# Layer three's weights applied in stage two of a graph network kernel

## The chip, the cores and the metric

The kernel runs on one core of a Trainium2 chip. The metric is the device time of one launch in microseconds. Three runs of the kernel before are given, and one profiled execution.

## The reference

There are 50000 nodes with 128 features and 100000 directed edges, sorted by their target, of which 50000 are the nodes' own loops. First h = relu(layernorm(x)) goes through three layers, and the result is added to x:

```
agg = segment_sum(h[src], dst) * inv_deg
h   = leaky_relu(agg @ Wl.T + b + h @ Wr.T, 0.01)
```

Then relu(layernorm(x)) goes through one attention layer: scores from two dot products, a softmax over the edges that enter a node, the weighted sum of the neighbours' rows, a bias, and again the residual. All is computed in float32. The edge attributes have no influence on the output.

## The kernel before

The nodes are cut into 196 tiles (NG) of 256 (TILE). After a preparation, which sorts out where each tile's edges lie and writes the first table of features to DRAM, four stages follow: layers one, two and three (`phase` with `ph` 1 and 2, then `phase_3`) and the attention (`phase_c`). Each stage runs once over the 196 tiles, and the next stage's gathers start only when all its table rows have been stored.

Every engine has its own program with the same loop over steps. In step s an engine handles several tiles, each at another point of its way; `s.at(-3)` is the tile three steps back. Semaphores count tiles. `steps(eng, 9, phase)` adds nine late steps in which the last tiles run out.

GpSimd gathers the source rows of the edges that are not loops, 128 rows by one indirect DMA (L635). Neighbouring tiles share a window of edges, so 417 gathers serve 196 tiles, at most twelve tiles ahead (DEEP). VectorE builds for each window a mask of 0 and 1 (L1247), edge by node, three tiles ahead. TensorE multiplies rows by mask (L852, `sums`), which gives the neighbours' sum transposed, feature by node. VectorE adds the tile's own transposed features (`with_own`, L1267) and multiplies by the inverse degree (`mean`, L1273), which SP has loaded from DRAM, copied to all partitions (L493). TensorE then multiplies by the two weight matrices of the layer (L877 and L878). A float32 product shows as two records (passes) in the trace, a transposition as one.

In stages one and two ScalarE adds the bias on the way out of PSUM (L722), VectorE applies the leaky relu (`leaky`, L1278), and TensorE transposes the tile back (L886). ScalarE copies that (L729) and stores both forms: `turned`, feature by node, for the next stage's own term, and `tab`, node by feature, for its gathers. SP loads the own term in stages two and three (L490).

Stage three computes the same sums (L852, L1267, L1273), but its products give node by feature: the bias as a product of three bfloat16 parts with ones (L913), then for each half of the tile the own term and the mean with the tile as the stationary operand (L917, L919). ScalarE copies the result (L747). VectorE applies the leaky relu (L1278), adds x (L1339), takes the layernorm's sums (`stats` L1203, `stats_end` L1212), the reciprocal (`scale`, L1219), adds the attention's bias for later (L1354) and prepares the shift nmr (`shift`, L1224). ScalarE takes the square root (`norm_scale`, L684) and applies the norm with the relu (`norm`, L691). TensorE transposes that (L928) and multiplies it by the attention's weights (L936), ScalarE copies both (L759, L765) and stores them as `tab_c` (L770). SP loads x (L477) and stores the sum x1 (L516).

In the attention stage the masks, scores and sums are built from the rows gathered from `tab_c`. It is changed in one thing only, the form in which x1 is loaded (L534). `pair_rows` lays two neighbouring nodes on a partition, so 1024 contiguous bytes; `node_rows` lays nodes p and p + 128 on partition p, so two pieces of 512 bytes.

Of the kernel before, what the change touches and what calls it, by code (L numbers as in the profile page):

```python
# [5 lines left out]
BF16 = mybir.dt.bfloat16  # L6
# [52 lines left out]
SP = 3  # L59
# [109 lines left out]
def build(nc, x, src, dst, wl1, bl1, wr1, wlh, blh, wrh, w_gat, att_s, att_d, bias, out):  # L169
# [11 lines left out]
    with ctx:  # L181
# [36 lines left out]
        ones_b = sb("ones_b", [P, P], BF16)  # L218
        b_part = sb("b_part", [SP, SP, D], BF16)
        b_rest = sb("b_rest", [SP, 2, D])  # L220
        b_sum = sb("b_sum", [SP, D])
        b_row = sb("b_row", [SP, 2, D], BF16)
        is_part = sb("is_part", [SP, SP])

# [67 lines left out]
        new_h = sage[:, 5632:6656].rearrange("p (r j d) -> p r j d", r=RING, j=2)  # L292
        act = sage[:, 3840:4352].rearrange("p (b j d) -> p b j d", b=2, j=2)
# [8 lines left out]
        mv = sb("mv", [P, 2, GJ, 2])  # L302
        std = sb("std", [P, 2, GJ])
# [54 lines left out]
        ps_agg = [None, bank[0:2], bank[0:3], bank[0:2]]  # L358
        ps_zz = [None, bank[3:5], bank[3:6], bank[3:5]]
        ps_own = [bank[2], bank[5]]  # L360
        ps_n = bank[6:8]
        ps_g = [bank[2], bank[5]]
# [4 lines left out]
        def pair(bk, w=D, stride=D):  # L367

            return bk[:, 0:2 * stride].rearrange("p (j w) -> p j w", j=2)[:, :, 0:w]
# [4 lines left out]
                 "sum_v t_v l_v z_a n_cp sq0 sq1 sq2 sq3 sq4 sq5 sq6 b_v ln_v ln_a rs_v nmr_v h_a tr_done ht_cp dense_done wg_done g_cp st0 st1 st2 "  # L374
# [4 lines left out]
                 "ge_v ge_a ge_m gn_v gn_a "  # L379
                 "gn_m low_g edge_st prep_seq turn_v turn_s chain_v chain_ps shift_g").split()  # L380
# [3 lines left out]
        main = [f"{n}{k}" for n, ring in (("ol", OWN), ("sq", OWN), ("il", RING), ("cl", RING)) for k in range(ring)]  # L384
        S.update((n, S[of]) for n, of in zip(general, main, strict=True))
# [19 lines left out]
        def kept(ph, t, ring):  # L405

            return (ph - 1) * NG + max(t - ring + 1, 0)

# [61 lines left out]
        def fast_sync(eng):  # L470
            def load_x(s):
                ld = S[f"x_ld{s.r}"]
                if s.last:
                    eng.dma_start(xin[0:TAIL // 2, s.r, :, :],
                                  x[N - TAIL:N, :].rearrange("(p j) d -> p j d", j=2)).then_inc(ld, 16)
                else:
                    eng.dma_start(xin[:, s.r, :, :], pair_rows(x, s.t)).then_inc(ld, 16)  # L477
# [1343 lines left out]
```

## Time and profile before

| | before |
|---|---|
| median of 3 runs | 2512.96 us |
| lowest and highest | 2511.53, 2515.49 us |
| span of the profiled execution | 2514.0 us |
| TensorE busy | 1865.3 us, 74% |
| VectorE busy | 1991.2 us, 79% |
| ScalarE busy | 1393.8 us, 55% |
| GpSimd busy | 1648.2 us, 66% |
| mean DMA rate | 232 GB/s |

The span of the profiled execution lies 1.0 us above the median. The shares are averages over stages with different limits, so they have to be read by stage. In the profile's lines the first number is the start in microseconds from the span's start, the next the duration; L852 is a line of the code; the text in brackets gives the idle time of the engine before the instruction, and what ended it.

### The profile page before, as it was taken

Reading aid. Unit: us, or ns where it says so; the run is one execution under the profiler, and the core shown is the slowest. Engines: PE = TensorE matmul, PEld = TensorE weight load, DVE = VectorE, ACT = ScalarE, POOL = GpSimd, SP = SyncE. Lnnn points to the kernel's source line nnn. Section 1 sums busy time; section 2 is a strip of 40 time slices with the busy share of each in tenths; the row PEclk is TensorE's granted clock in tenths of the full one; section 3 lists DMA queues with packets and bytes.
Section 4 is the critical chain, followed back from the end, with each engine's and each line's share of the span. In section 5 each row is a group of like instructions: output and inputs, shape, how many; then the busy total and the mean of one; then the engine's idle time right before and its main releaser. Section 6 shows DMA issues by size and latency. Waiting matters only on the chain. (4 is left out here: it accounts for less than half of the span.)

```text
span 2514.0 us, 49419 instructions
## 1 busy us (share of the span) xinstructions
PE 1865.3 (74%) x12376; PEld 1627.8 (65%) x12376; DVE 1991.2 (79%) x8222; ACT 1393.8 (55%) x3711; POOL 1648.2 (66%) x1706
## 2 busy tenths in 40 slices
PE   0000888888886887888887999999999566666666
PEld 0000777777775777777766888888888456555555
DVE  7988766666664666666656999999999699999999
ACT  3696344444442222222223666666666688888887
POOL 2002777777775777777766777767672577777774
PEclk9999999999998999999998999999999799999998
DMA  6685788888886888888886988888888588887887
GB/s 207 216 296 204 235 249 245 247 249 246 249 248 180 244 253 244 244 251 242 251 231 200 264 263 261 258 256 255 257 256 234 139 205 204 206 202 202 205 203 174
DMA packets 597881, 582.84 MB, mean 232 GB/s; under 512 B 79531, under 2 KB 557349, under 8 KB 597568
## 3 DMA queue, kind: packets, MB, share of 16 engines
q1 hardware_dynamic: 402272, 337.58, 44.7%
q0 software_dynamic: 54208, 112.76, 21.0%
q10 hardware_dynamic: 141120, 129.32, 15.0%
q8 instruction: 107, 1.75, 0.3%
q14 instruction: 174, 1.43, 0.2%
HBM read 372.40 MB, written 207.75 MB: 231 GB/s over the span
## 5 line engine op out<-in xcount | busy, mean ns | idle before, releaser
L635 POOL DMA_INDIRECT rows<-tab,idx x1251 | 1229.4, 983 | 548.7 <-issue 342.6
L852 PE MATMUL bank<-mask,rows 128*128 128x128 f32 (+1 forms) x3528 | 645.6, 320 | 208.9 <-DMA rows<-tab,idx 185.9
L852 PEld LDWEIGHTS bank<-mask,rows 128*128 128x128 f32 x3528 | 543.9, 195 | 286.4 <-issue 165.6
L1267 DVE TENSOR_TENSOR sage<-bank,sage 128x256 f32<-128x256 f32 x588 | 247.2, 420 | 413.2 <-PE bank L852 410.9
L722 ACT ACTIVATE sage<-bank,b_col 128x256 f32<-128x256 f32 x392 | 185.9, 474 | 599.6 <-PE bank L878 599.1
L635 POOL DMA_INDIRECT rows<-tab_c,idx x417 | 398.1, 955 | 181.5 <-issue 115.8
L1247 DVE TENSOR_SCALAR mask<-iota,dcol 128x256 f32<-128x256 f32 (+1 forms) x1251 | 418.8, 365 | 0.1
L953 PE MATMUL bank<-ident,mask 128*128 128x128 f32 x784 | 139.9, 305 | 177.5 <-ACT mask L782 176.8
L1273 DVE TENSOR_TENSOR sage<-sage 128x256 f32<-128x256 f32 x588 | 246.3, 419 | 1.8 <-DMA sage<-inv_d 1.6
L1278 DVE SCALAR_TENSOR_TENSOR sage<-sage 128x256 f32<-128x256 f32 x588 | 243.0, 413 | 4.6 <-ACT sage L722 4.6
L877 PE MATMUL bank<-sage,wcat 128*128 128x256 f32 x784 | 236.9, 384 | 0.0
L878 PE MATMUL bank<-sage,wcat 128*128 128x256 f32 x784 | 236.0, 383 | 0.0
L953 PEld LDWEIGHTS bank<-ident,mask 128*128 128x128 f32 x784 | 90.8, 151 | 208.1 <-ACT mask L782 195.2
L963 PE MATMUL bank<-rows,sage 128*128 128x131 f32 x1568 | 224.3, 290 | 1.4 <-ACT sage L802 1.4
L782 ACT ACTIVATE mask<-cut_w,rows 128x256 f32<-128x256 bf16 (+1 forms) x417 | 181.0, 484 | 61.1 <-issue 39.0
L963 PEld LDWEIGHTS bank<-rows,sage 128*128 128x128 f32 x1568 | 207.6, 205 | 1.6 <-ACT sage L802 1.6
L691 ACT ACTIVATE sage<-sage,nmr,rstd 128x128 f32<-128x128 f32 x392 | 172.2, 486 | 42.9 <-DVE nmr L1224 41.6
L802 ACT ACTIVATE sage<-cut_w,ed 128x256 f32<-128x256 bf16 (+1 forms) x441 | 184.4, 473 | 4.9 <-DVE ed L1475 2.6
L917 PE MATMUL bank<-wcat,sage 128*128 128x128 f32 x784 | 177.3, 308 | 0.0
L886 PEld LDWEIGHTS bank<-ident,sage 128*128 128x128 f32 x784 | 152.9, 196 | 22.8 <-issue 4.9
L878 PEld LDWEIGHTS bank<-sage,wcat 128*128 128x128 f32 x784 | 150.9, 192 | 20.9
L1450 DVE TENSOR_REDUCE mx<-bank 128x2 f32<-128x512 f32 x196 | 132.7, 677 | 33.8 <-PE bank L953 33.4
(219 smaller groups left out, 3276.9 us busy)
## 6 DMA issues: line engine op xcount, KB each, us to landing
sage<-inv_d SPq DMA_DIRECT2D x588, 128.0 KB
turned<-sage ACTq DMA_DIRECT2D x392, 128.0 KB
tab<-sage ACTq DMA_DIRECT2D x392, 128.0 KB
sage<-turned SPq DMA_DIRECT2D x392, 128.0 KB
tab_c<-sage ACTq DMA_DIRECT2D x196, 132.0 KB
own_w<-tab_c SPq DMA_DIRECT2D x196, 132.0 KB, 2.9
tab<-sage SPq DMA_DIRECT2D x49, 512.0 KB, 3.5
xin<-tab SPq DMA_DIRECT2D x196, 128.0 KB
```

Of the source, the lines that this page charges most:

```text
L635: eng.indirect_dma_start(out=rows[:, s.win[w], 0:width], out_offset=None, in_=table, in_offset=bass.IndirectOffsetOnAxis(ap=idx[:, s.w + w ...
L722: eng.activation(new_t[:, o.v, :], ps_zz[ph][o.t % len(ps_zz[ph])][:, 0:TILE], ACT.Identity, bias=b_col[:, ph - 1:ph]).then_inc(S["z_a"], 1)
L802: m = eng.activation(prob[:, o.mw[w], a:b], cut[:, o.win[w], a:b], ACT.Exp, bias=ed[:, o.g, 2 * o.k + w:2 * o.k + w + 1])
L852: m = eng.matmul(to[:, a:b], rows[:, s.win[w], 0:D], mask[:, s.mw[w], c:c + b - a], start=(w == 1), stop=(w == 2))
L877: eng.matmul(to, wcat[:, ph - 1, D:2 * D], own_t[:, o.v, :], start=True, stop=False)
L878: eng.matmul(to, wcat[:, ph - 1, 0:D], agg_t[:, o.r, :], start=False, stop=True).then_inc(S["dense_done"], 1)
L953: m = eng.transpose(ps_z[s.t % 3][:, j * TILE + n * P:j * TILE + (n + 1) * P], score[:, s.mw[j + n], (1 - n) * P:(2 - n) * P], ident[:, :])
L963: m = eng.matmul(ps_o[o.k][:, j * TILE:j * TILE + D + 3], prob[:, o.mw[j + n], (1 - n) * P:(2 - n) * P], rows[:, o.win[j + n], 0:D + 3], s ...
L1247: m = eng.tensor_scalar(to[:, g.mw[w], a:b], io[:, a:b], node, None, ALU.is_equal)
L1267: eng.tensor_tensor(agg_t[:, o.r, :], ps[:, 0:TILE], own_t[:, o.v, :], ALU.add).then_inc(S["sum_v"], 1)
L1273: eng.tensor_tensor(agg_t[:, o.r, :], agg_t[:, o.r, :], inv_b[:, o.r, :], ALU.mult).then_inc(S["t_v"], 1)
L1278: eng.scalar_tensor_tensor(at, at, 0.01, at, ALU.mult, ALU.max).then_inc(S["l_v"], 1)
```

## The change

The mean and the product with a matrix can be exchanged, and so can the leaky relu and a multiplication by a positive number. The change uses both for layer three.

At the end of stage two each tile is multiplied by both of layer three's matrices at once, with the tile as the stationary operand (two float32 products of 256 columns), in place of the two transpositions. The half that belongs to Wl is copied by ScalarE and stored as the table for stage three's gathers. VectorE (`weigh`) takes the half that belongs to Wr, adds the bias, multiplies by the degree and adds the tile's own Wl half (the loop). ScalarE stores this one step later to `turned`.

Stage three then starts a PSUM bank with a product of the identity and this prepared term, and adds the gathered rows with the masks as the stationary operand, four products of 128 columns. The result is the layer's value before the leaky relu, times the degree. VectorE applies the leaky relu and, in one operation for each half, multiplies by the inverse degree and adds x. The sums by `with_own`, the multiplication by `mean`, the load of the inverse degree, the bias product and the four products with weights are gone from this stage, and its tiles run through fewer steps: ScalarE has 8 late steps in place of 11. The degree and its inverse, node by partition, are prepared once between stages one and two, by four transpositions, a copy and a reciprocal. The bias parts that stood between stages two and three go. Stage two's table, x and `tab_c` move by `node_rows`, x1 is loaded by `pair_rows`. The diff, cut to its core (lines between @@ say where a piece stands):

```
+        w_out = sage[:, 6656:8448].rearrange("p (v j d) -> p v j d", v=OWN, j=2)
...
-        ps_agg = [None, bank[0:2], bank[0:3], bank[0:2]]
-        ps_zz = [None, bank[3:5], bank[3:6], bank[3:5]]
+        ps_agg = [None, bank[0:2], bank[0:3]]
+        ps_zz = [None, bank[3:5], bank[3:5]]
...
-        ps_g = [bank[2], bank[5]]
+        ps_p = bank[5:8]
+        ps_y = bank[0:4]
+        ps_g = bank[4:6]
...
@@ SP, load(g) of a tile: @@
-                    wait(eng, S["t_v"], kept(ph, g.t, RING))
-                    eng.dma_start(inv_b[:, g.r, :], inv_d[g.t, :].partition_broadcast(P)
-                                  ).then_inc(S[f"il{g.r}"], 16)
+                    if ph < LAYERS:
+                        wait(eng, S["t_v"], kept(ph, g.t, RING))
+                        eng.dma_start(inv_b[:, g.r, :], inv_d[g.t, :].partition_broadcast(P)
+                                      ).then_inc(S[f"il{g.r}"], 16)
+                    else:
+                        wait(eng, S["x1_v"], g.t - RING + 1)
+                        load_x(g)
...
@@ ScalarE, stages one and two: @@
-                        eng.activation(new_h[:, o.r, :, :], pair(ps_n[o.b], D, D), ACT.Copy).then_inc(S["n_cp"], 1)
-                        store_t(o, ph, S["l_v"])
+                        of = pair(ps_n[o.b], D, D) if ph == 1 else pair(ps_p[o.t % len(ps_p)], D, TILE)
+                        eng.activation(new_h[:, o.r, :, :], of, ACT.Copy).then_inc(S["n_cp"], 1)
+                        if ph == 1:
+                            store_t(o, ph)
                     if s.at(-9).there:
-                        store_h(s.at(-9), ph, S["n_cp"])
-                steps(eng, 9, phase)
+                        store_h(s.at(-9), ph)
+                    if ph > 1 and s.at(-10).there:
+                        store_t(s.at(-10), ph)
+                steps(eng, 9 if ph == 1 else 10, phase)
...
@@ ScalarE, stage three (the copy of the result, then the order of norm and norm_scale): @@
-                o = s.at(-4)
+                o = s.at(-1)
...
-                if s.at(-5).there:
-                    norm_scale(s.at(-5), NSG + s.t - 5)
-                o = s.at(-6)
+                o = s.at(-3)
                 if o.there:
                     wait(eng, S["tr_done"], ka + o.t - 1)
                     norm(o, NSG + o.t, h_c[:, o.b, :, :], x1, o.r)
-                o = s.at(-8)
+                if s.at(-2).there:
+                    norm_scale(s.at(-2), NSG + s.t - 2)
+                o = s.at(-5)
...
-            steps(eng, 11, phase_3)
+            steps(eng, 8, phase_3)
...
@@ TensorE, stage two: @@
+                            wait(eng, S["w_v"], o.t - len(ps_p) + 1)
+                            for j in range(2):
+                                m = eng.matmul(ps_p[o.t % len(ps_p)][:, j * TILE:(j + 1) * TILE], new_t[:, o.v, j * P:(j + 1) * P],
+                                               wcat[:, LAYERS - 1, :], start=True, stop=True)
...
@@ TensorE, stage three: @@
-                    sums(s, LAYERS)
-                o = s.at(-3)
-                if o.there:
-
-                    own_there(eng, o, LAYERS)
-                    eng.wait_ge(S["t_v"], ka + o.t + 1)
-                    eng.wait_ge(S["z_a"], kept(LAYERS, o.t, 2))
-                    to = ps_zz[LAYERS][o.b]
-                    eng.matmul(to[:, 0:TILE], ones_b[0:SP, :], b_row[:, :, :].rearrange("p j d -> p (j d)"),
-                               start=True, stop=False)
+                    own_there(eng, s, LAYERS)
+                    wait(eng, S["z_a"], kept(LAYERS, s.t, len(ps_y)))
+                    to = ps_y[s.t % len(ps_y)]
+                    eng.matmul(to[:, 0:TILE], ident[:, :], own_t[:, s.v, :], start=True, stop=False)
+                    eng.wait_ge(S["mask_done"], ka + s.t + 1)
+                    rows_there(eng, s, LAYERS)
                     for j in range(2):
-                        of_j = to[:, j * D:(j + 1) * D]
-                        eng.matmul(of_j, own_t[:, o.v, :].rearrange("p (n j) -> p j n", j=2)[:, j, :],
-                                   wcat[:, LAYERS - 1, D:2 * D], start=False, stop=False)
-                        m = eng.matmul(of_j, agg_t[:, o.r, :].rearrange("p (n j) -> p j n", j=2)[:, j, :],
-                                       wcat[:, LAYERS - 1, 0:D], start=False, stop=(j == 1))
-                    m.then_inc(S["dense_done"], 1)
+                        for n in range(2):
+                            m = eng.matmul(to[:, j * D:(j + 1) * D], mask[:, s.mw[j + n], (1 - n) * P:(2 - n) * P],
+                                           rows[:, s.win[j + n], 0:D], start=False, stop=(j == 1 and n == 1))
+                    m.then_inc(S["agg_done"], 1)
...
@@ VectorE, stage two, for the tile nine steps back, after leaky: @@
+            def weigh(f):
+                eng.wait_ge(S["n_cp"], NG + f.t + 1)
+                eng.tensor_tensor(t_b[:, f.b, :, :], pair(ps_p[f.t % len(ps_p)], D, TILE, D),
+                                  b_bc[:, LAYERS - 1, :].unsqueeze(1).to_broadcast([P, 2, D]), ALU.add
+                                  ).then_inc(S["b_v"], 1)
+                eng.wait_ge(S["b_v"], f.t + 1)
+                wait(eng, S[f"sq{f.v}"], 16 * (NG // OWN + f.uses(OWN)))
+                for j, n in enumerate(of_node(deg_n, f.t)):
+                    m = eng.scalar_tensor_tensor(w_out[:, f.v, j, :], t_b[:, f.b, j, :], n, new_h[:, f.r, j, :],
+                                                 ALU.mult, ALU.add)
+                m.then_inc(S["w_v"], 1)
...
@@ VectorE, stage three: @@
-                if o.there:
-                    with_own(o, LAYERS)
...
-                    leaky(act[:, f.b, :, :])
                 mask_part(s.at(3), LAYERS, 0)
+                    eng.scalar_tensor_tensor(y, y, 0.01, y, ALU.mult, ALU.max).then_inc(S["y_v"], 1)
+                mask_part(s.at(3), LAYERS, 1)
...
-                    eng.tensor_tensor(x1[:, f.r, :, :], act[:, f.b, :, :], xin[:, f.r, :, :], ALU.add
-                                      ).then_inc(S["x1_v"], 1)
-                mask_part(s.at(3), LAYERS, 1)
-                if o.there:
-                    mean(o, LAYERS)
+                    for j, n in enumerate(of_node(inv_n, f.t)):
+                        m = eng.scalar_tensor_tensor(x1[:, f.r, j, :], act[:, f.b, j, :], n, xin[:, f.r, j, :],
+                                                     ALU.mult, ALU.add)
+                    m.then_inc(S["x1_v"], 1)
+                mask_part(s.at(3), LAYERS, 2)
...
-            steps(eng, 6, phase_3)
+            steps(eng, 3, phase_3)
```

## Rows read from the trace of the kernel before

**Rows 1.** The page's 40 slices of the span, tenths of busy time by engine.

```profile
DVE  7988766666664666666656999999999699999999
...
POOL 2002777777775777777766777767672577777774
```

**Rows 2.** Timeline of GpSimd at stage ends: start, us, instruction, [idle before it <-releaser].

```profile
785.04 0.94 POOL L635 DMA_INDIRECT rows<-tab,idx  x1 [16.81 <-DMA tab<-sage]
...
1311.76 0.94 POOL L635 DMA_INDIRECT rows<-tab,idx  x1 [0.30 <-issue]
1329.98 1.08 POOL L635 DMA_INDIRECT rows<-tab,idx  x1 [17.27 <-DMA tab<-sage]
...
1909.89 0.96 POOL L635 DMA_INDIRECT rows<-tab,idx  x1 [0.30 <-issue]
1965.61 0.94 POOL L635 DMA_INDIRECT rows<-tab_c,idx  x1 [54.76 <-DMA tab_c<-sage]
```

**Rows 3.** Windows: stretch, length, busy by engine (PE, PEld, DVE, ACT, POOL), clock, DMA, GB/s.

```profile
850.00:1300.00 450.00, 366.73 (x2007) 321.38 (x2007) 282.67 (x857) 125.54 (x335) 341.81 (x356) 0.97 0.86 247
1350.00:1450.00 100.00, 98.47 (x668) 84.28 (x667) 97.08 (x418) 59.41 (x178) 75.71 (x80) 1.00 0.86 247
1650.00:1850.00 200.00, 199.55 (x1339) 169.29 (x1338) 194.81 (x837) 127.06 (x384) 140.78 (x136) 1.00 0.88 256
```

**Rows 4.** The sums' line L852 on TensorE, stage two, then three: ns, first and last.

```profile
L852 PE MATMUL bank<-mask,rows x1176: 272/275/767, 791.2 to 1317.7; 128*128 128x256 f32 x196
...
L852 PE MATMUL bank<-mask,rows x1176: 272/275/767, 1336.3 to 1944.6; 128*128 128x256 f32 x196
```

**Rows 5.** Timeline of TensorE, a tile of stage two, then of stage one.

```profile
999.93 1.04 PE L852 MATMUL bank<-mask,rows 128*128 128x256 f32 x6
1000.81 0.60 PE L877 MATMUL bank<-sage,wcat 128*128 128x256 f32 x2
1001.24 0.59 PE L878 MATMUL bank<-sage,wcat 128*128 128x256 f32 x2
...
760.17 0.39 PE L886 MATMUL bank<-ident,sage 128*128 128x128 f32 x2
760.40 0.38 PE L866 MATMUL bank<-ident,xin 128*128 128x128 f32 x2
```

**Rows 6.** Timeline of TensorE, a tile of stage three.

```profile
1655.14 0.41 PE L928 MATMUL bank<-ident,sage 128*128 128x128 f32 x2
1655.41 0.69 PE L936 MATMUL bank<-wg,sage 128*128 128x130 f32 x4
1655.94 0.71 PE L852 MATMUL bank<-mask,rows 128*128 128x256 f32 x3
```

**Rows 7.** Timeline of VectorE, a tile of stage three.

```profile
1653.68 0.41 DVE L1267 TENSOR_TENSOR sage<-bank,sage 128x256 f32<-128x256 f32 x1
1654.02 0.41 DVE L1278 SCALAR_TENSOR_TENSOR sage<-sage 128x256 f32<-128x256 f32 x1
1654.51 0.42 DVE L1339 TENSOR_TENSOR sage<-sage,xin 128x256 f32<-128x256 f32 x1
1654.85 0.36 DVE L1247 TENSOR_SCALAR mask<-iota,dcol 128x256 f32<-128x256 f32 x1
```

**Rows 8.** Timeline of VectorE, attention stage.

```profile
2102.83 0.34 DVE L1463 SCALAR_TENSOR_TENSOR sage<-sage,rden 128x128 f32<-128x128 f32 x1
2103.09 0.35 DVE L1469 SCALAR_TENSOR_TENSOR sage<-sage,rden 128x128 f32<-128x128 f32 x1
```

**Rows 9.** Timeline of ScalarE, stage three.

```profile
1650.31 0.30 ACT L684 ACTIVATE std<-mv,eps 128x2 f32<-128x2 f32 x1 [0.91 <-DVE mv L1212]
1650.81 0.49 ACT L691 ACTIVATE sage<-sage,nmr,rstd 128x128 f32<-128x128 f32 x1 [0.21 <-DVE nmr L1224]
```

**Rows 10.** DMA queues: packets, MB, share; attention stage (2050:2450), then stage two (850:1300).

```profile
q1 hardware_dynamic: 122201, 59.53, 54.2%
...
q10 hardware_dynamic: 48022, 43.73, 28.0%
```

More of the change, by code:

```diff
@@ L407, in kept, with of_node @@
             return (ph - 1) * NG + max(t - ring + 1, 0)
+        def of_node(a, t):
+            u, q = t // 2, t % 2
+            return [a[:, 2 * q + j, u:u + 1] for j in range(2)]
         def node_rows(a, t):
@@ L508, in phase @@
                             load(g)
-                    g = s.at(-2)
-                    if ph == LAYERS and g.there:
-                        wait(eng, S["x1_v"], g.t - RING + 1)
-                        load_x(g)
-                    o = s.at(-6)
+                    o = s.at(-4)
                     if ph == LAYERS and o.there:
@@ L893, in fast_tensor @@
                     eng.wait_ge(S["oc_a"], NG)
+                    for q in range(2):
+                        for j in range(2):
+                            at = (2 * q + j) * HALF
+                            m = eng.transpose(ps_deg[:, at:at + HALF], deg[:, q, j * P:(j + 1) * P], ident[0:HALF, 0:HALF])
+                    m.then_inc(S["dn_ps"], 1)
                     eng.wait_ge(S["sum_v"], NG)
                     eng.wait_ge(S["z_a"], NG)
+                    eng.wait_ge(S["dn_v"], 1)
             ka = (LAYERS - 1) * NG
@@ L1299, in phase @@
                         leaky(new_t[:, f.v, :])
-                steps(eng, 5, phase)
-            for k in range(SP):
-                op(eng.tensor_scalar(is_part[:, k:k + 1], part[0:SP, 0:1], float(k), None, ALU.is_equal))
-            op(eng.tensor_copy(b_rest[:, 0, :], b_bc[0:SP, LAYERS - 1, :]))
-            for k in range(SP):
-                op(eng.tensor_copy(b_part[:, k, :], b_rest[:, k % 2, :]))
-                if k < SP - 1:
-                    op(eng.tensor_tensor(b_rest[:, (k + 1) % 2, :], b_rest[:, k % 2, :], b_part[:, k, :], ALU.subtract))
-            op(eng.tensor_scalar(b_sum[:, :], b_part[:, 0, :], is_part[:, 0:1], None, ALU.mult))
-            op(eng.scalar_tensor_tensor(b_sum[:, :], b_part[:, 1, :], is_part[:, 1:2], b_sum[:, :], ALU.mult, ALU.add))
-            op(eng.scalar_tensor_tensor(b_sum[:, :], b_part[:, 2, :], is_part[:, 2:3], b_sum[:, :], ALU.mult, ALU.add))
-            op(eng.tensor_copy(b_row[:, 0, :], b_sum[:, :]))
-            eng.tensor_copy(b_row[:, 1, :], b_sum[:, :]).then_inc(S["b_v"], 1)
+                    f = s.at(-9)
+                    if ph > 1 and f.there:
+                        weigh(f)
+                if ph > 1:
+                    eng.wait_ge(S["dn_ps"], 1)
+                    op(eng.tensor_copy(deg_n[:, :, :].rearrange("p k u -> p (k u)"), ps_deg[:, 0:4 * HALF]))
+                    op(eng.reciprocal(inv_n[:, :, :], deg_n[:, :, :]))
+                    eng.sem_inc(S["dn_v"], 1)
+                steps(eng, 5 if ph == 1 else 9, phase)
             for r in range(RING):
```

113 lines of the change are left out of this document (60 added, 53 removed).

## The prediction

> **What bounds the kernel now.** I read the page's slices first, then busy time by stage, then the first and last instruction of the queues that could carry a stage, then single steps. The slices show four stretches after the preparation: three stages of the convolution and the attention stage; VectorE is at 6 tenths in the first two and at 9 in the last two, GpSimd at 7 in all but the third, where it falls to 6 [rows 1]. A stage handles 196 tiles with 417 gathers. In stage two the first gather starts at 785.04 and the last at 1311.76 [rows 2]: 526.7 us for 417, 1.266 us each, 2.69 us a tile. One gather takes 0.94 us and the next follows 0.30 us later with nothing to wait for [rows 2], so GpSimd's issue rate sets this stage; TensorE is busy for 366.7 of 450 us, VectorE for 282.7 [rows 3]. TensorE's sums run from 791.2 to 1317.7 [rows 4], 2.70 us a tile, six microseconds behind the gathers.
>
> Stage three is different. Early in it (1350 to 1450) 80 gathers still run in 100 us, but from 1650 to 1850 only 136 in 200 us, while TensorE is busy for 199.55 of 200 us and VectorE for 194.8 [rows 3]. The sums run from 1336.3 to 1944.6 [rows 4], 608.3/195 = 3.12 us a tile: TensorE sets the pace. Behind it stands a drain: the last gather starts at 1909.89, the attention stage's first at 1965.61 after 54.76 us of idle time that the stores of tab_c ended [rows 2]; 34.7 us of this are the backlog and 21.0 us (1944.6 to 1965.6) the run through the late steps.
>
> **TensorE in stage three.** A tile costs now 3.12 us. The change drops the bias product, the four products with layer three's weights (eight passes of 128 columns) and the three sums. It puts in a product of ident with the own term (two passes of 256 columns) and four products mask by rows (eight passes of 128). A product of two 256-column passes takes 0.43 us (1000.81 to 1001.24) [rows 5]; four passes of 128 or 130 columns take 0.53 us (1655.41 to 1655.94), the two transposes 0.27 us before it [rows 6]. New tile, added up: 0.43 + 1.06 (8 × 0.53/4) + 0.27 + 0.53 = 2.29 us. By subtraction from the measured step: 3.12 less 0.88 for the sums (999.93 to 1000.81) [rows 5], 1.06 for the eight passes and 0.21 for the bias (one pass of 256 columns, half of 0.43), plus 0.43 and 1.06: 2.46. Either is under 2.69, so the gathers become the bound.
>
> **VectorE in stage three.** Busy 194.8/200 × 3.12 = 3.04 us a tile [rows 3]. Removed: the PSUM addition L1267 (0.34, to the start of L1278), the multiplication by the inverse degree L1273 (the same shape, 0.34), and the residual addition L1339 (0.34); the 0.49 us between the start of the activation L1278 and L1339 holds 0.15 us of waiting for its result [rows 7], which two masks in between can hide. Added: two multiply-adds of 128 columns; the same form with a pointer scalar starts every 0.26 us in the attention stage (2102.83 to 2103.09) [rows 8], 0.52 us. Sum: 3.04 − 1.02 + 0.52 = 2.54, or 2.39 with the wait gone. Under 2.69, by little.
>
> **ScalarE and the shortened pipeline.** Its work a tile stays (five activations). But its norm now stands ahead of norm_scale of the next tile, and VectorE's shift needs that norm_scale one step later: a loop. Its length: 0.21 from VectorE's nmr to the first norm, at most 2 × 0.49 for the norms, 0.30 for the square root [rows 9], some 0.2 back, and 0.4 for the reciprocal and a 256-column addition (priced as L1267), about 2.1 us. Under 2.69, so I charge nothing. SP now fetches x two tiles ahead of its use and issues own_t behind a wait for x1_v; what is queued behind that wait is the next own_t, needed about three tiles (8 us) later. Nothing charged.
>
> **DMA in stage three.** At 3.12 us a tile and 256 GB/s it moves 799 KB [rows 3]. The copies of the inverse degree (131 KB) go: 668 KB, at 2.69 us 248 GB/s, less than now. Against it, x and tab_c now move in 512- and 528-byte pieces. q1 in the attention stage took 0.542 × 16 × 400 us / 122201 = 28.4 ns for 487 bytes, q10 in stage two 0.280 × 16 × 450 / 48022 = 42.0 ns for 911 bytes [rows 10]; 128 KB in halves is then 256 × 28.4 against 128 × 42.0 ns, 1.9 us more over 16 engines, 0.12 us a tile and transfer. I take no loss of pace; the upper bound is a rival.
>
> Stage three then: 195 × (3.12 − 2.70) = 82 us less in its steady part. The drain has eight late steps in place of eleven; 21.0 us becomes about 17 (bounds 13 and 21). Together **86 us less** (bounds 80 and 91).
>
> **Stage two pays.** TensorE: today 0.88 for the sums, 0.43 and 0.43 for the dense products, 0.23 for two transposes (760.17 to 760.40) [rows 5], 1.97 us. The two transposes become two fp32 products of 256 columns: 1.97 − 0.23 + 0.86 = 2.60 us. VectorE: today 282.7/450 × 2.70 = 1.70 us [rows 3]; weigh adds a 256-column addition from PSUM with a wait for its own result (0.49, as from L1278 to L1339 [rows 7]) and two 128-column multiply-adds (0.52 [rows 8]): 2.71 us. ScalarE keeps two activations and two stores. So three engines now need 2.60, 2.71 and 2.69 us a tile, where one did. The lower bound of the pace is 2.70, no loss; the upper one is 3.0, two more waits of 0.15 us on VectorE on top of 2.71, because weigh also waits for ScalarE's copy and for an old store. I take 2.76, near the slowest engine: 195 × 0.06 = 12 us. The drain gets one step and VectorE's weigh, which the third product back waits for: +3 us on today's 12.3 (1317.7 to 1329.98) [rows 2, 4]. Its third buffer for ps_p costs ps_zz one; dense then waits for ScalarE's copy two tiles back, a step behind. The store of w_out waits for w_v on ScalarE, and the next tile's activation is queued behind it; it is one VectorE step late and covered by two buffers. Nothing charged. Together **15 us more** (bounds 3 and 62).
>
> **Edges at nothing.** The degree's four transposes, copy and 392-column reciprocal stand between stages one and two, where TensorE's first sum of stage two starts 6 us after the first gather (791.2 against 785.04) [rows 2, 4]: up to 3 us hide there. The bias splitting between two and three goes; it lay under the 17.27 us in which GpSimd waited for stores [rows 2], and the rows still come 6 us later. The first own_t is needed at once in stage three; its load runs while the first rows are fetched. The attention stage loads x1 in larger pieces, but is held by its gathers; nothing.
>
> **The sum.** The profiled execution's span is 2514.0 us, 1.0 above the median of the three times, 2512.96. 2514.0 − 86 + 15 = 2443 for such an execution, 2442 as a median.
>
> **A rule that speaks against it.** In stage three's early part the gathers keep 1.25 us each (75.71 us busy for 80) while VectorE is busy for 97.1 of 100 us [rows 3], so a full VectorE did not slow them. The Trainium skill, page "SBUF — State Buffer", section "SBUF: two separate sides", says that VectorE and GpSimd share one pair of ports as a lock, and that descriptors of GpSimd's DMAs can wait for it. Stage two gets three more VectorE operations a tile, two of them with two SBUF inputs, and by that rule its gathers could slow; the trace disagrees so far.
>
> **Rivals.**
> 1. Three full engines in stage two get in each other's way: 3.0 us a tile, 195 × 0.30 + 3 = 62 more in place of 15: 2489. For: 2.60, 2.71 and 2.69 leave no reserve, and waits of VectorE on ScalarE's copy come in. Against: in stage three now two engines run 99.8% and 97% busy together [rows 3]. Chance 0.13.
> 2. The gathers slow, by the lock or by DMA. Small pieces raise DMA's share of 0.88 × 3.12 = 2.75 us a tile less 0.33 for the inverse degree (128 × 42 ns/16) plus 0.24, to 2.66 in 2.69: nearly full. A gather took 0.95 us in early stage three and 1.04 late (75.71/80, 140.78/136) [rows 3]; +0.09 on 834 gathers is 75 us at most, half of it 38: 2481. Against: 248 GB/s is no more than now. Chance 0.13.
> 3. **Slower**: the loop VectorE, ScalarE, VectorE of stage three decides. Today ScalarE takes the square root ahead of its norm; the change puts it behind, so scale of the next tile may find it late. VectorE works in order: it then stands still, and its 2.54 us follow the wait instead of lying beside it. ScalarE's part of the loop is 0.21 + 0.98 + 0.30 = 1.5 us [rows 9]; with 0.65 of it uncovered the step is 3.2 us, and 195 × 3.2 + 21 + 6 = 651 us lie between the first gather and the next stage's in place of 635.6: with stage two's 15, 2544. It decides from 3.04 us a tile on (195 × 3.04 + 27 = 635.6 − 15). For: scale is reached only some 2 us after the shift that lets the norm go (2.54 less the 0.5 for addition and shift). Against: these 2 us are more than 1.5. Chance 0.05.
> 4. Stage two stays at the gathers' pace and the drain is short: 2514 − 91 + 3 = 2426. Chance 0.09.
> That the products keep being the bound in stage three (the mask as weights costing more than counted) would need 0.4 us beyond 2.29; it is inside the forecast's upper end.
>
> **How the numbers follow.** Forecast 0.60, the rivals as above. 8 times in 10 the time lies between 2422 (rival 4 with a little) and 2488 (just short of rival 1). Faster by over 0.2% (5 us, about what a measurement can tell): all but rival 3, 0.94; within 0.2%, 0.01; slower, 0.05.
>
> **What would show it.** Stage three's 136 gathers per 200 us become about 158, with TensorE under 95% busy and its waits ended by the rows' DMA; the idle time of GpSimd ahead of the attention stage falls from 54.76 to about 22 us. Stage two's TensorE and VectorE go to 95% and more, its gathers from 526.7 to about 535 us, and some of them wait for TensorE. I am wrong if stage two's pace passes 2.9, if stage three's is over 2.8, or if its gathers have a mean over 1.0 us.

## The result, and the profile after

The changed kernel takes 2499.68 us, median of 4 runs (2496.79 to 2504.22), the kernel before in the same series 2514.22 (2511.53 to 2517.24): ratio 0.9946, 95% interval 0.9934 to 0.9958. It is faster by 0.5%, where 2442 us, 2.9% less, was forecast and 2422 to 2488 was the range. The profiled execution's span is 2494.8 us.

Two of the page's 40 slices: busy tenths of VectorE and GpSimd in the changed kernel.

```profile
DVE  7988766666665999999997888888888599999999
POOL 2002777777775777777775777777772677777774
```

Against [rows 1] VectorE has gone from 6 to 9 in stage two and from 9 to 8 in stage three. The timeline of GpSimd at the stage ends answers to [rows 2]: start, duration, instruction, idle time before it and what ended it.

```profile
1319.11 0.94 POOL L641 DMA_INDIRECT rows<-tab,idx  x1 [0.30 <-issue]
1340.34 0.94 POOL L641 DMA_INDIRECT rows<-tab,idx  x1 [20.29 <-DMA tab<-sage]
...
1897.80 1.03 POOL L641 DMA_INDIRECT rows<-tab,idx  x1 [0.30 <-issue]
1945.24 0.95 POOL L641 DMA_INDIRECT rows<-tab_c,idx  x1 [46.42 <-DMA tab_c<-sage]
```

Measured from the first gather of a stage to that of the next (785.0, 1330.0 and 1965.6 before; 784.3, 1340.3 and 1945.2 after), stage two went from 544.9 to 556.1 us and stage three from 635.6 to 604.9. Stage one (552.2 to 551.8) and the attention stage (548.4 to 549.6) stayed. So stage two paid 11 us, about as forecast, and stage three gave back 31 instead of 86.

The windows of the changed kernel answer to [rows 3]: stretch, length, busy by engine (PE, PEld, DVE, ACT, POOL), clock, DMA, GB/s.

```profile
850.00:1300.00 450.00, 436.41 (x2303) 382.09 (x2302) 424.09 (x1338) 141.36 (x329) 343.39 (x350) 1.00 0.87 244
1350.00:1450.00 100.00, 77.14 (x536) 66.34 (x536) 85.53 (x412) 60.84 (x193) 76.19 (x79) 0.98 0.79 217
1650.00:1850.00 200.00, 156.03 (x1066) 138.62 (x1064) 168.62 (x810) 125.25 (x401) 140.32 (x143) 0.97 0.82 225
```

In the third row no engine is full: TensorE 156 of 200 us, VectorE 169, DMA at 0.82. Yet only 143 gathers ran, where 158 were forecast. The first and last record of the stage's products, from the view of one line, answer to [rows 4]: the pace is (1930.4 − 1346.3)/195 = 3.00 us a tile, and the run-out 1945.2 − 1930.4 = 14.8 us.

```profile
L946 PE MATMUL bank<-rows,mask x1568: 272/275/551, 1346.3 to 1930.4; 128*128 128x128 f32 x196
```

What every engine waited for between 1650 and 1850 (engine, line, releaser: us in total, times, longest):

```profile
ACT sage L697 <- DVE nmr L1249: 74.5, 66, 3.3
PEld bank L955 <- ACT sage L697: 46.5, 39, 3.0
PE bank L955 <- ACT sage L779: 43.2, 51, 2.8
POOL rows L641 <- issue: 33.7, 110, 0.4
DVE sage L1384 <- DMA x_d<-sage: 31.1, 40, 2.7
POOL rows L641 <- PE bank L946: 26.1, 33, 2.6
```

ScalarE waits for VectorE (nmr), TensorE for ScalarE, GpSimd for TensorE: a chain of waits that all lead to VectorE, and VectorE waits for a store, x_d<-sage. 168.62 busy plus 31.1 waiting are its whole 200 us. Over the whole stage the form view gives that wait 93.5 us, 0.48 a tile, and 3.00 less 0.48 is 2.52 us, VectorE's work.

```profile
L1384 DVE TENSOR_TENSOR sage<-sage,b_bc 128x256 f32<-128x256 f32 x196 | 82.1, 419 | 95.5 <-DMA x_d<-sage 93.5
```

L1384 writes x1b, the layer's result plus the attention's bias (L1354 before). x1b has two buffers, so L1384 needs the store of the tile two back. In the kernel before nothing waited for that store, which SP issued 0.44 us after the start of L1354:

```profile
1690.87 0.40 DVE L1354 TENSOR_TENSOR sage<-sage,b_bc 128x256 f32<-128x256 f32 x1
1691.31 0.34 SPq L516 DMA_DIRECT2D x_d<-sage  x1
```

The timelines of SP's issues (SPq) and of VectorE in the changed kernel show why it is late now:

```profile
1693.07 0.42 DVE L1384 TENSOR_TENSOR sage<-sage,b_bc 128x256 f32<-128x256 f32 x1 [0.22 <-DMA x_d<-sage]
1694.21 0.60 DVE L1373 SCALAR_TENSOR_TENSOR sage<-sage,inv_n,xin 128x128 f32<-128x128 f32 x2
1694.84 0.38 SPq L483 DMA_DIRECT2D xin<-in_x  x1
1695.27 0.53 SPq L522 DMA_DIRECT2D x_d<-sage  x1
...
1695.39 0.42 DVE L1384 TENSOR_TENSOR sage<-sage,b_bc 128x256 f32<-128x256 f32 x1
1696.72 0.61 DVE L1373 SCALAR_TENSOR_TENSOR sage<-sage,inv_n,xin 128x128 f32<-128x128 f32 x2
1697.79 0.47 SPq L522 DMA_DIRECT2D x_d<-sage  x1
...
1699.52 0.42 DVE L1384 TENSOR_TENSOR sage<-sage,b_bc 128x256 f32<-128x256 f32 x1 [1.47 <-DMA x_d<-sage]
...
1702.44 0.42 DVE L1384 TENSOR_TENSOR sage<-sage,b_bc 128x256 f32<-128x256 f32 x1 [0.45 <-DMA x_d<-sage]
```

x1b is written at 1693.07 and could be stored from 1693.5 on. But SP works in order: it first waits for VectorE's residual addition L1373 of the next step (x1_v, the end at 1694.81), fetches x (L483, 1694.84) and only then issues the store (L522, 1695.27). The buffer is wanted at 1698.05 (1699.52 less 1.47), 2.8 us later; the store lands 4.25 us after its issue. At 2.70 us a tile a store has 0.12 + 2.70 = 2.8 us (1695.27 to 1695.39, and a step). The one issued at 1692.58 came within 2.81 us (L1384 at 1695.39 does not wait), this one cost 1.47, and the next, issued at 1697.79, landed after 4.65. The Trainium skill, page "DMA: Bandwidth & Descriptors", section "Anatomy of one DMA — SWDGE (gpsimd) path", says that a DMA's semaphore wait is kept on the issuing sequencer and that a transfer has some 2 us of fixed time, mostly the confirmation of the write; it describes GpSimd's path, and this store is SP's. The order of these rows agrees with the first; the landings of 4.25 and 4.65 us are about twice the second.

### The profile page after: what moved, and what is told of

Read it like the earlier page. It is cut to its first block and busy times, and to the rows that moved or that the text cites. A ratio compares the mean times of both kernels' runs of the same rounds, so it can differ in the third digit from the quotient of the medians.

```text
span 2494.8 us, 48242 instructions
## 1 busy us (share of the span) xinstructions
PE 1802.6 (72%) x11792; PEld 1589.4 (64%) x11792; DVE 2062.2 (83%) x8601; ACT 1394.6 (56%) x3711; POOL 1647.4 (66%) x1706
## 5 line engine op out<-in xcount | busy, mean ns | idle before, releaser
L872 PE MATMUL bank<-mask,rows 128*128 128x128 f32 (+1 forms) x2352 | 425.1, 318 | 114.2 <-DMA rows<-tab,idx 93.8
L872 PEld LDWEIGHTS bank<-mask,rows 128*128 128x128 f32 x2352 | 369.0, 193 | 182.1 <-issue 114.0
L1272 DVE TENSOR_SCALAR mask<-iota,dcol 128x256 f32<-128x256 f32 (+1 forms) x1251 | 407.5, 357 | 0.3
L1292 DVE TENSOR_TENSOR sage<-bank,sage 128x256 f32<-128x256 f32 x392 | 165.8, 423 | 228.2 <-PE bank L872 225.3
L946 PEld LDWEIGHTS bank<-rows,mask 128*128 128x128 f32 x1568 | 214.5, 200 | 31.5 <-issue 13.5
L946 PE MATMUL bank<-rows,mask 128*128 128x128 f32 x1568 | 217.8, 284 | 14.3 <-DMA rows<-tab,idx 10.0
L913 PE MATMUL bank<-wcat,sage 128*128 128x256 f32 x784 | 200.9, 379 | 0.0
L745 ACT ACTIVATE sage<-bank 128x256 f32<-128x256 f32 x392 | 149.1, 380 | 77.8 <-PE bank L913 75.6
L955 PE MATMUL bank<-ident,sage 128*128 128x128 f32 x392 | 82.2, 293 | 121.5 <-ACT sage L779 119.5
L1298 DVE TENSOR_TENSOR sage<-sage 128x256 f32<-128x256 f32 x392 | 164.9, 421 | 2.9 <-DMA sage<-inv_d 2.6
```

Source lines behind the costliest of these rows:

```text
L872: m = eng.matmul(to[:, a:b], rows[:, s.win[w], 0:D], mask[:, s.mw[w], c:c + b - a], start=(w == 1), stop=(w == 2))
L913: m = eng.matmul(ps_p[o.t % len(ps_p)][:, j * TILE:(j + 1) * TILE], new_t[:, o.v, j * P:(j + 1) * P], wcat[:, LAYERS - 1, :], start=True, ...
L946: m = eng.matmul(to[:, j * D:(j + 1) * D], mask[:, s.mw[j + n], (1 - n) * P:(2 - n) * P], rows[:, s.win[j + n], 0:D], start=False, stop=(j ...
L1272: m = eng.tensor_scalar(to[:, g.mw[w], a:b], io[:, a:b], node, None, ALU.is_equal)
```

## The experiments

Theory A: the store of x1b, queued in SP behind the wait for x1_v, sets stage three's pace. Rival B: the loop of VectorE and ScalarE (norm ahead of norm_scale; rival 3 of the prediction in a milder form), of which the store is only a symptom. Rival C: DMA is full with smaller pieces, so stores and gathers are late wherever they are issued.

In the first series, the four runs that follow, all engines stood still together now and then in every stage of every kernel, the one before included (2888.33 us, about 3.26 us a tile); it tells only about differences that are large against that, and no total expected for it (2440 to 2460 us for either mend) could be met. The table has stage lengths between first gathers, and stage three's pace; the experiments of the later series are beside it.

| kernel | time, us | stage one | two | three | attention | pace of three |
|---|---|---|---|---|---|---|
| before | 2514.22 | 552.2 | 544.9 | 635.6 | 548.4 | 3.12 |
| changed | 2499.68 | 551.8 | 556.1 | 604.9 | 549.6 | 3.00 |
| first series: store first | 2881.4 | 656.4 | 657.4 | 667.0 | 666.3 | 3.31 |
| first series: four buffers | 2879.9 | 657.7 | 657.6 | 668.0 | 661.9 | 3.31 |
| first series: store a step late | 3233.37 | 655.7 | 656.1 | 1022.8 | 664.4 | 5.13 |
| first series: square root first | 2892.86 | 657.5 | 659.3 | 671.0 | 668.7 | |
| changed, again | 2508.7 | 552.5 | 558.1 | 615.1 | 550.6 | 3.04 |
| square root first, again | 2512.43 | 550.5 | 557.9 | 616.7 | 552.9 | 3.06 |
| four buffers, again | 2447.17 | 552.8 | 559.7 | 551.2 | 549.3 | 2.73 |
| store first, again | 2447.39 | 551.6 | 557.9 | 552.5 | 550.3 | 2.73 |
| store and square root first | 2446.84 | 552.6 | 556.4 | 554.1 | 548.4 | 2.74 |
| store first, no bias | 2442.2 | 552.4 | 550.2 | 552.1 | 553.0 | 2.74 |
| store first, half product | 2438.89 | 552.1 | 553.1 | 552.4 | 547.2 | 2.73 |
| store first, bias early | 2443.82 | 551.8 | 553.8 | 553.6 | 550.1 | 2.74 |

**Store first** (two buffers, the store ahead of the loads in SP's step):

```
+                    o = s.at(-4)
+                    if ph == LAYERS and o.there:
+                        eng.wait_ge(S["x1b_v"], o.t + 1)
+                        eng.dma_start(pair_rows(x1_d, o.t), x1b[:, o.b, :, :]).then_inc(...)
                     for g in ahead(s, 2):
                         if g.there:
                             load(g)
-                    o = s.at(-4)
-                    ...
```

> The changed kernel with SP's store of x1b issued ahead of the loads of the same step instead of behind them, buffers left at two. Theory A: the store is issued about one operation of VectorE's step plus two issues of SP (0.4 us each) earlier, at least 1 us and up to a whole step; the wait at L1384 (31 us of 200) goes nearly all, pace 2.70-2.80, span 2440-2460. Theory B and C: no change, span 2485-2505.

**Four buffers** (the store stays where the change has it):

```
-        x1b = sage[:, 5376:5888].rearrange("p (b j d) -> p b j d", b=2, j=2)
+        x1b = sage[:, 1792:2816].rearrange("p (r j d) -> p r j d", r=RING, j=2)
...                              (the store, its semaphores and L1384 count four buffers)
```

> The changed kernel with one edit: x1b, which VectorE writes and SP stores to x1_d, has four buffers in place of two. Theory A (the store of x1b: VectorE's addition L1384 waits for the store of two tiles back, which SP issues only behind its wait for x1_v): the 0.5 us a tile of that wait go, stage three's pace falls from 3.00 to 2.70-2.75 us a tile, stage three takes about 550 us instead of 604.9, span about 2440-2450 us. Theory B (the loop VectorE's nmr, ScalarE's norm, then square root, VectorE's scale sets the pace, and the store is only what is seen last): pace stays within 2.9-3.0 and the span within 10 us of 2495, the wait only moves to L1244 or ScalarE's L690. Theory C (DMA in 512-byte pieces is full): pace stays near 3.0 and rows' DMA become what TensorE waits for.

**Store a step late** (one line, and one late step more):

```
-                    o = s.at(-4)
+                    o = s.at(-5)
...
-                steps(eng, 4 if ph == LAYERS else 0, phase)
+                steps(eng, 5 if ph == LAYERS else 0, phase)
```

> The changed kernel with SP's store of x1b issued one step later (five steps back instead of four), buffers left at two. Theory A: nearly the whole time of the store, 2 to 2.5 us, now stands in VectorE's way in each tile: pace about 5 us, stage three some 950-1050 us, span 2850-2950. Theory B and C: the store has slack, and the pace rises by less than 0.5 us a tile, span under 2600.

**Square root first** (ScalarE's order as in the kernel before):

```
+                if s.at(-2).there:
+                    norm_scale(s.at(-2), NSG + s.t - 2)
                 o = s.at(-3)
                 if o.there:
                     ...
-                if s.at(-2).there:
-                    norm_scale(s.at(-2), NSG + s.t - 2)
```

> The changed kernel with ScalarE's square root (norm_scale, L690) put back ahead of its norm (L697), as in the kernel before. Theory B: pace falls towards 2.7, span 2440-2460. Theory A: VectorE still waits for the store at L1384, pace 2.95-3.1, span 2485-2520; it may get worse, since the norm then waits for the end of VectorE's step.

Measured in this series: 2881.4, 2879.9 (ratio to before 0.9973, interval 0.9961 to 0.9984), 3233.37 and 2892.86 us. Stage three of the mended kernels is 667 and 668 us, of the one with ScalarE's order alone 671. That is little, since every stage here ran at about 3.3 us a tile, so a store had 3.4 us to land. The late store decides: the pace becomes 5.13 us in stage three alone, and the stage 1022.8 us, within the 950 to 1050 that theory A gave (the total, 3233.37 us, is beyond its 2950, since the other stages are longer too). The waits of that kernel between 1700 and 2150, then a step of its timelines of SP and VectorE:

```profile
DVE sage L1384 <- DMA x_d<-sage: 224.0, 88, 4.5
```

```profile
1904.52 0.61 DVE L1373 SCALAR_TENSOR_TENSOR sage<-sage,inv_n,xin 128x128 f32<-128x128 f32 x2
1905.16 0.38 SPq L483 DMA_DIRECT2D xin<-in_x  x1
1905.59 0.47 SPq L522 DMA_DIRECT2D x_d<-sage  x1
1908.46 0.43 DVE L1384 TENSOR_TENSOR sage<-sage,b_bc 128x256 f32<-128x256 f32 x1 [2.60 <-DMA x_d<-sage]
1909.60 0.61 DVE L1373 SCALAR_TENSOR_TENSOR sage<-sage,inv_n,xin 128x128 f32<-128x128 f32 x2
```

The closed loop can be read off: 1.07 us from L1373 to the store, 2.87 for the landing, 1.14 from L1384 to the next L1373, 5.08 together. Theory A foretold such a loop; B and C allowed less than 0.5 us a tile.

A second series, without those pauses (before 2515.06 us, 2512.34 to 2520.64), repeated the changed kernel and three of the edits.

> The changed kernel itself, once more, because in the runs before these every kernel, the one before among them, ran at about 3.26 us a tile in each stage with pauses of all engines at once. Where those pauses are absent: 0.9946 of the kernel before, stage three at 3.00 us a tile with VectorE waiting some 0.5 us a tile at L1384 for the store of x1b. Where they are there: stage three within 1% of its variants, and nothing can be told from it.

> The changed kernel with four buffers of x1b in place of two. Theory A (VectorE's wait for the store of x1b two tiles back sets stage three's pace): 2.70-2.75 us a tile, 50 to 57 us less than the changed kernel on the same chip, 0.971-0.976 of the kernel before. Theory B (the loop of VectorE and ScalarE): within 10 us of the changed kernel. Theory C (DMA is full): pace near 3.0, TensorE waits for rows.

> The changed kernel with the store of x1b issued ahead of the same step's loads, two buffers. Theory A: VectorE's wait at L1384 goes nearly all, pace 2.70-2.80, 40 to 57 us less than the changed kernel. Theories B and C: as the changed kernel.

> The changed kernel with ScalarE's square root ahead of its norm again. Theory B: pace falls towards 2.7, 40 to 57 us less. Theory A: as the changed kernel or up to 20 us more, VectorE still waits at L1384.

The changed kernel took 2508.7 us (7 runs; ratio 0.9972, interval 0.9960 to 0.9983; 0.9946 was expected, so its gain is half as large here), and its L1384 waited 103.0 us for the store, four buffers 2447.17 (4 runs; 0.9724, interval 0.9706 to 0.9742), store first 2447.39 and square root first 2512.43 (one run each). Either mend alone takes 61 us off (57 was the most that theory A gave) and brings stage three from 615.1 to 551 or 552.5 us; L1384's wait for the store is then 2.5 us (store first) or none (four buffers). The windows of four buffers, and its waits from 1650 to 1850:

```profile
1350.00:1450.00 100.00, 78.41 (x547) 69.33 (x548) 87.51 (x423) 63.23 (x197) 76.49 (x78) 0.94 0.81 226
1650.00:1850.00 200.00, 168.02 (x1172) 149.10 (x1171) 185.64 (x894) 139.86 (x442) 151.92 (x158) 0.94 0.88 246
```

```profile
POOL rows L641 <- issue: 46.9, 153, 0.3
ACT sage L697 <- DVE nmr L1249: 35.1, 58, 0.7
PE bank L946 <- DMA rows<-tab,idx: 28.6, 27, 3.3
```

158 gathers, TensorE waiting for rows: what the prediction said would show it. C falls: the same pieces move at 246 GB/s, more than the 225 of the changed kernel. In store first two steps of the timelines show the store leaving as soon as x1b is there:

```profile
1691.27 0.40 DVE L1384 TENSOR_TENSOR sage<-sage,b_bc 128x256 f32<-128x256 f32 x1
1691.70 0.34 SPq L519 DMA_DIRECT2D x_d<-sage  x1
1692.39 0.61 DVE L1373 SCALAR_TENSOR_TENSOR sage<-sage,inv_n,xin 128x128 f32<-128x128 f32 x2
1693.02 0.38 SPq L483 DMA_DIRECT2D xin<-in_x  x1
```

0.43 us after L1384, so 2 × 2.7 − 0.4 = 5.0 us to land in place of 2.8. Square root first alone leaves VectorE's wait for the store (36.7 us in this stretch): its waits from 1650 to 1850 say

```profile
ACT std L690 <- DVE mv L1237: 79.1, 65, 3.4
...
DVE sage L1384 <- DMA x_d<-sage: 36.7, 39, 2.6
```

so B falls here, as its stage three (616.7 against 615.1) already says. Whether the loop is late next, once the store is mended, was asked by itself:

> Based on the version with the store of x1b ahead of SP's loads; ScalarE takes the square root of the next tile ahead of the norm in stage three, as the kernel before did. Theory: the loop VectorE, ScalarE, VectorE is about 2.1 us and shorter than the 2.7 us of a tile, so stage three stays at 550 to 555 and the total at 2446 to 2449. Rival: once the store's wait is gone the loop is what is late next; then VectorE's wait at the reciprocal is over 20 us in 200 without this edit, and with it stage three becomes 5 to 10 us shorter.

It took 2446.84 us, stage three 554.1: the loop is not late next either.

**Stage two.** Three kernels on top of store first ask which engine sets its 2.75 us (its pace in the six kernels that keep stage two as the change has it: 2.737 to 2.760). No bias, which leaves layer three's bias out; its two multiply-adds then read one input from PSUM in place of SBUF:

```
-                eng.tensor_tensor(t_b[:, f.b, :, :], pair(ps_p[f.t % len(ps_p)], D, TILE, D), ..., ALU.add
-                                   ).then_inc(S["b_v"], 1)
-                eng.wait_ge(S["b_v"], f.t + 1)
...
-                    m = eng.scalar_tensor_tensor(w_out[:, f.v, j, :], t_b[:, f.b, j, :], n, ...
+                    m = eng.scalar_tensor_tensor(w_out[:, f.v, j, :], pair(ps_p[...], D, TILE, D)[:, j, :], n, ...
```

> Based on the version with the store of x1b ahead of SP's loads. In stage two weigh's two multiply-adds read PSUM directly; the addition of layer three's bias and the wait for its result are left out, so that bias is missing from the result. The question is which engine sets stage two's pace (2.75 us a tile, 417 gathers, stage length 556 to 560). VectorE theory: it loses 0.49 us a tile, so the pace falls to the gathers' 2.70 and the stage to 546 to 550 (drain 0.5 shorter); total 2436 to 2440. TensorE theory: nothing in its work changes, the pace stays 2.74 to 2.76 and the stage 556 to 559; total 2446 to 2448. Gathers theory (they are a little slower when all engines are busy): stage unchanged too, GpSimd's waits for TensorE few in both.

Half product, which leaves the product with Wr out; `weigh` reads the Wl half in its place:

```
-                                m = eng.matmul(ps_p[...][:, j * TILE:(j + 1) * TILE], new_t[...],
-                                               wcat[:, LAYERS - 1, :], start=True, stop=True)
+                                m = eng.matmul(ps_p[...][:, j * TILE:j * TILE + D], new_t[...],
+                                               wcat[:, LAYERS - 1, 0:D], start=True, stop=True)
```

> Based on the version with the store of x1b ahead of SP's loads. Stage two's product with layer three's matrices is made with the Wl half alone (128 columns in place of 256), and weigh reads that half twice; the Wr product is left out. TensorE loses 0.43 us a tile (2.60 to 2.17), VectorE nothing. TensorE theory: the pace falls to 2.70 and stage two to 546 to 550; total 2436 to 2440. VectorE theory: stage two stays at 556 to 559; total 2446 to 2448.

Bias early, the best version that computes all:

```
+                    if ph > 1 and s.at(-9).there:
+                        add_bias(s.at(-9))
                     (the step's masks)
                     ...
                     weigh(s.at(-9))        (now the two multiply-adds alone)
```

> Based on the version with the store of x1b ahead of SP's loads; in stage two VectorE adds the bias ahead of the step's masks and does the multiply-adds where they were, so the masks lie in the 0.15 us wait between them. Nothing is left out. If VectorE's 2.71 us a tile set stage two's pace, it falls from 2.75 to about 2.70 and the total to 2438 to 2442; if TensorE or the gathers set it, stage two stays at 556 to 559 and the total at 2446 to 2448. Slower rival: the bias addition now stands ahead of the mask and waits for TensorE's product, so the mask comes later and the pace rises over 2.80.

Without the bias addition the pace is 2.710 and the stage 550.2 us; with half the product 2.734 and 553.1, of which 1.6 us are the run-out (13.5 in place of 15.1). The windows of the two, no bias and then half product:

```profile
850.00:1300.00 450.00, 439.38 (x2334) 388.80 (x2334) 364.44 (x1189) 143.58 (x334) 341.82 (x355) 1.00 0.88 247
```

```profile
850.00:1300.00 450.00, 389.94 (x2306) 347.98 (x2305) 417.12 (x1336) 135.62 (x328) 343.30 (x351) 0.98 0.86 244
```

TensorE relieved of 0.3 us a tile (390 of 450 us busy): the pace stays, and TensorE's waits for rows rise from 13.3 to 54.4 us of the 450. VectorE relieved (364 of 450): the pace falls by 0.03 to 0.05 us. This looks as if VectorE's 2.71 us set the pace, but GpSimd's own waits in the changed kernel's stage two (850 to 1300) say otherwise:

```profile
POOL rows L641 <- issue: 97.8, 321, 0.3
POOL rows L641 <- PE bank L872: 8.9, 29, 0.3
```

No wait is longer than 0.3 us, the gap that stands between any two gathers. Over all of stage two, in the ten traces outside the first series, the gaps beyond 0.31 us add up to 0.1 us at most. So nothing holds GpSimd, and stage two keeps the pace of its gathers, as before the change; TensorE's last sums start 6.1 us behind the last gather (5.9 before). What has changed is how long a gather takes, from a mean of 0.960 to 0.981 us. From the first to the last gather are 534.8 us against 526.7, and that is the whole of the 8.1 us that the steady part pays. With no bias the mean is 0.965 and this stretch 528.6 us; with half the product 0.979 and 534.3; with the bias early 0.976 and 533.3; in the six kernels 0.981 to 0.989 and 534.8 to 538.8.

How long a gather takes goes with the moment at which VectorE's operations fall on it. In the changed kernel's stage two the gathers that start 0.14 to 0.16 us ahead of the multiplication by the inverse degree (L1298, both inputs in SBUF) take 1.04 to 1.06 us, all seven, and those that start 0.25 to 0.29 us ahead take 0.94 to 0.95, all five; no bias shows the same two figures. Six gathers take over 1.6 us, where the kernel before has one and no bias and bias early have none. Each begins 0.05 to 0.12 us ahead of L1298, with the leaky relu L1303 right behind it:

```profile
842.54 1.68 POOL L641 DMA_INDIRECT rows<-tab,idx  x1 [0.30 <-issue]
842.66 0.41 DVE L1298 TENSOR_TENSOR sage<-sage 128x256 f32<-128x256 f32 x1
842.99 0.41 DVE L1303 SCALAR_TENSOR_TENSOR sage<-sage 128x256 f32<-128x256 f32 x1
```

The five more of these make some 3.5 of the 8.1 us (an estimate from their durations). Six other gathers at 0.12 us took 1.00 to 1.01, so what else such a long one needs is open, and no run changed the place of these operations alone. That VectorE's work lengthens the gathers, and by that sets the pace, is what the traces suggest; that the pace follows the gathers is what they show.

The totals that were expected do not decide here (no bias and half product are one run each). No bias (2442.2 us) and bias early (2443.82) lie in neither theory's range, and half product (2438.89) in the one for TensorE, although its pace says the opposite. Stages that no edit touches differ by several us from trace to trace: stage two 556.1 to 559.7, the attention stage 547.2 (half product) to 553.0 (no bias). Of the three, only no bias, 6 us under the lowest, stands well out of that. Bias early (4 runs, 2441.3 to 2446.2; ratio to before, 2515.54 in this series, 0.9717, interval 0.9701 to 0.9733) has an interval that overlaps that of four buffers, so it is not shown to be faster than that one.

## Why the prediction was wrong

**The step that failed** is in "ScalarE and the shortened pipeline": "what is queued behind that wait is the next own_t, needed about three tiles (8 us) later. Nothing charged." The list was short by one. Behind SP's wait for x1_v stands also the store of x1b, which SP issues after the loads of its step. In the kernel before, x was fetched for a tile four steps older than that, so its wait was long met and the store went out 0.44 us after its data. The change fetches x earlier, by the same count of x1_v, and the wait is now met one VectorE step later than the store's own. Its price is 0.48 us a tile, 93.5 us of VectorE's time in the stage; in the second series 103.0 us, and there 61 us of the whole between changed and mended kernels (2508.7 against 2447.2). The 61 are less than the 103, since VectorE, at 2.53 us of work in a pace of 2.73, would otherwise have stood some 0.2 us a tile. The prediction's own sign of being wrong, a pace of over 2.8 in stage three, came true.

**Stage three.** The rest of its sum held, once the store was mended. The pace is 2.73 (forecast 2.70), the run-out 12.4 to 12.6 us (17 forecast, with bounds of 13 and 21, so it was put too long), the stage 551 to 552.5 us, so 83 to 84 less than 635.6 where 86 was forecast. VectorE's work is 168.62/200 × 3.00 = 2.53 us a tile in the changed kernel (2.54); TensorE's 156.03/200 × 3.00 = 2.34 (2.29 to 2.46). The run-out of 14.8 us in the changed kernel still had the store in it.

**Stage two.** 15 us more were forecast, 11 measured, 12 to 15 in the later series. The sizes of the engines' steps held, but they did not set the pace, so the nearness of 2.76 forecast to 2.74 measured is in part luck. TensorE's step, start to start of the sums, is 2.61 us in its timeline (2.60 forecast), and has the parts of the sum (0.88, 0.43, 0.43 and 0.87 us):

```profile
1001.18 1.04 PE L872 MATMUL bank<-mask,rows 128*128 128x256 f32 x6
1002.06 0.60 PE L897 MATMUL bank<-sage,wcat 128*128 128x256 f32 x2
1002.49 0.59 PE L898 MATMUL bank<-sage,wcat 128*128 128x256 f32 x2
1002.92 1.03 PE L913 MATMUL bank<-wcat,sage 128*128 128x256 f32 x4
1003.79 1.04 PE L872 MATMUL bank<-mask,rows 128*128 128x256 f32 x6
```

VectorE is busy for 424.09/450 × 2.74 = 2.58 us; with the 0.15 us that the prediction gave to the wait for its own result, 2.73 (2.71). But it was the gathers that took 1.286 us each from start to start (534.8/416), 2.74 us a tile. The prediction left them at 1.266 us, added 0.06 us a tile with VectorE's 2.71 as the slowest engine, and expected some gathers to wait for TensorE; the gathers became 0.02 us longer instead and waited for nobody. The run-out grew by 2.8 us, from 12.3 to 15.1 (3).

**The rivals.** Rival 1 (3.0 us in stage two) did not come. Rival 2 (slower gathers) came in a small form: a gather in stage two took 0.98 us (343.39/350) with VectorE 94% busy, against 0.96 (341.81/356) at 63% before, and these 0.02 us are the 8 us of the steady part, not the 38 of the rival. The stretch that the prediction held against it (75.71 us for 80 gathers beside a full VectorE) does not rule it out, since the length goes by the moment at which an operation falls on a gather, not by the busy share. The rule of the Trainium skill, page "SBUF — State Buffer", section "SBUF: two separate sides", of a lock between VectorE and GpSimd, agrees with the gathers' lengths beside L1298 in its direction; that this lock is their cause is not shown. Rival 3 had the mechanism's form, a wait that opens VectorE's full step, but put it in ScalarE; two kernels show that this order costs nothing. Its threshold of 3.04 us a tile was nearly reached by the store (3.00 and 3.04). Edges and the attention stage, charged with nothing, moved by at most 1.2 us in the runs of the result.

## What to carry to other kernels

When a load is moved earlier in an in-order queue, write down every instruction that this queue issues after it in the same step, stores above all, and for each one the time from its new issue to the reuse of its buffer. A store in two buffers has one step and a little to land; here 2.8 us were too few at a pace of 2.7, and 5.0 were enough. Where no engine is full afterwards and the gain is missing, look for the engine whose busy time and waits together fill the window, ask what releases it, and test that with an edit to the releaser alone. And before an engine at 97% is called the bound, look at the gaps of the one that feeds it: here the feeder never waited, it had become slower.

## What the runs showed of the hardware

The time from the start of a store's issue on SP (128 KB to DRAM) to the release of the engine that waits for it varies: 4.25 and 4.65 us for two neighbouring stores of the changed kernel, where one just before them took at most 2.81; with the store a step late a median of 2.7 us, from 2.1 to 4.7, over the 88 waits between 1700 and 2150, where DMA carried 132 GB/s. What makes one late is open. Where buffers leave a store 2.8 us, this decides: the changed kernel differed by 9 us between two series (2499.68 and 2508.7), with 10 of them in stage three (604.9 and 615.1).

In stage two TensorE ran for 450 us at 97% busy with a granted clock of 1.00, the higher of its two levels (2.4 GHz). A gather that GpSimd issues takes 1.04 to 1.06 us when VectorE's L1298 starts 0.14 to 0.16 us after it, and 0.94 to 0.95 when that starts 0.25 to 0.29 us after it, while the gap to the next gather stays 0.30 us.
